# A graph and expert kernel on one core: GpSimd's row sum waits for one more VectorE step, and VectorE's list rows come ahead of its search

## What is computed

```python
x = x + _L0_gnn_ref(_layernorm(x), edge_index, ...)     # 8 heads of 64
x = x + _L0_ffn_ref(_layernorm(x)[None], ...)[0]        # 8 experts, top 1
x = x + _L1_gnn_ref(_layernorm(x), edge_index, W, b)
x = x + _L1_ffn_ref(_layernorm(x)[None], ...)[0]        # 64 experts

# end of the first graph step, for each node and head:
out = segment_sum(w[:, :, None] * x_l[src], dst)  # listed edges + the node's own loop
return elu(out + bias) + x
# first feed-forward step, for each node:
h = relu(xf @ W1[e] + b1[e]);  oe = h @ W2[e] + b2[e]
out = out + where(idx_k == e, gate_k * oe, 0.0)   # only the best expert's h counts
```

## Time and profile before

| | us |
|---|---|
| median of 3 runs | 2760.67 |
| lowest, highest | 2751.52, 2766.61 |
| profiled execution, its own time | 2749.01 |
| its span from first to last instruction | 2747.3 |
| first and last start of the wide sum L1072 | 1000.5, 1376.7 |

### The profile page before, as it was taken

The page is one execution under the profiler, slowest core; times in us unless marked ns, Lnnn a source line. Parts: engine busy times, 40 slices in busy tenths (PEclk is TensorE's granted clock), DMA queues, the critical chain, the costliest instruction groups (busy, mean ns, idle before and its releaser), DMA issues. The chain is left out here.

```text
span 2747.3 us, 43544 instructions
## 1 busy us (share of the span) xinstructions
PE 2127.1 (77%) x11528; PEld 1264.7 (46%) x11554; DVE 1834.1 (67%) x5188; ACT 928.1 (34%) x2017; POOL 1791.9 (65%) x2144
## 2 busy tenths in 40 slices
PE   8999999957777739999978969999997577774000
PEld 3444444435555526666644436666664344442000
DVE  5776676645555569999951126777778487776666
ACT  1111111115555515777764425555554000000000
POOL 3555555477777457888727745777777655664776
PEclk9999999978998959999989989999999799997555
DMA  6655555548999756888749976766663799997999
GB/s 199 230 192 179 185 192 181 183 155 280 309 305 306 245 160 199 254 262 265 244 164 361 403 270 206 213 218 218 216 212 104 229 358 382 373 352 257 381 385 353
DMA packets 361541, 699.30 MB, mean 255 GB/s; under 512 B 51513, under 2 KB 85139, under 8 KB 361297
## 3 DMA queue, kind: packets, MB, share of 16 engines
q1 hardware_dynamic: 239816, 399.95, 42.6%
q0 software_dynamic: 76720, 218.39, 24.3%
q10 hardware_dynamic: 44761, 78.17, 7.9%
HBM read 426.08 MB, written 287.44 MB: 260 GB/s over the span
## 5 line engine op out<-in xcount | busy, mean ns | idle before, releaser
L2119 POOL DMA_INDIRECT xg<-n_rows,ids x219 | 219.0, 1000 | 126.4 <-PE psum L154 78.4
L148 PE MATMUL psum<-wl,xT 128*128 128x512 f32 x632 | 288.8, 600 | 0.0
L148 PE MATMUL psum<-wg,yT 128*128 128x512 f32 x632 | 285.2, 594 | 0.0
L148 PE MATMUL psum<-wr,xT 128*128 128x512 f32 x632 | 284.1, 592 | 0.0
L337 ACT ACTIVATE xb<-xa,xsc 128x512 f32<-128x512 f32 x79 | 64.4, 817 | 479.6 <-POOL xsc L397 479.6
L154 PE MATMUL psum<-ident,xg 128*128 128x128 f32 x876 | 139.4, 298 | 103.9 <-DVE gT L2226 88.8
L384 POOL TENSOR_TENSOR ve<-mv,epst 128x1 f32<-128x1 f32 x79 | 51.0, 646 | 254.4 <-DVE mv L439 254.4
L1688 POOL DMA_INDIRECT slot_tokens<-sl x158 | 169.0, 1070 | 70.6 <-issue 66.9
L2285 POOL DMA_INDIRECT q<-slot_outputs,qs x158 | 165.1, 1045 | 72.0 <-issue 47.8
L148 PEld LDWEIGHTS psum<-wr,xT 128*128 128x128 f32 x632 | 120.1, 190 | 151.2 <-issue 151.2
L148 PE MATMUL psum<-wc,x1T 128*128 128x264 f32 x632 | 162.8, 402 | 32.1 <-DVE hb L1231 24.6
(11 more groups left out here) (322 smaller groups left out, 5329.1 us busy)
## 6 DMA issues: line engine op xcount, KB each, us to landing
slot_outputs<-yo ACTq DMA_DIRECT2D x54, 1024.0 KB
x_rows<-x SPq DMA_DIRECT2D x158, 256.0 KB, 3.2
edge_sums<-eo SPq DMA_DIRECT2D x29, 1056.0 KB, 6.7
edge_sums<-go SPq DMA_DIRECT2D x29, 1024.0 KB
xT<-in_xTt SPq DMA_DIRECT2D x79, 256.0 KB
xl_rows<-xl SPq DMA_DIRECT2D x79, 256.0 KB
xr_rows<-xr SPq DMA_DIRECT2D x79, 256.0 KB
residual_rows<-xb SPq DMA_DIRECT2D x79, 256.0 KB, 3.8
```

Source lines behind the costliest of these rows:

```text
L148: last = nc.tensor.matmul(ps, lhs[:, k, :], rhs[:, k, :], start=(k == 0), stop=(k == DK - 1))
L2119: pool.indirect_dma_start(xg[:, t % 8, :], None, XN3, bass.IndirectOffsetOnAxis(ids[:, t:t + 1], 0), bounds_check=NP - 1, oob_is_err=False ...
```

## The change

`average` gets a wait: from tile 9 on, the sum of tile t waits until `routed` of tile t-9 is through. Both VectorE steps, `self_part` of tile t and `routed` of tile t-9, belong to VectorE's turn t+2. And in VectorE's list `listed_part` moves from behind `best` to ahead of it, and `best` moves ahead of the two group steps `larger` and `slopes`. No instruction is added or taken away on any engine.

```diff
@@ average
                     pool.wait_ge(c_ta, t + 1)
                     pool.wait_ge(c_ts, t + 1)
+                    if t >= 9:
+                        pool.wait_ge(c_hm, t - 8)
                     if t >= 3:
                         pool.wait_ge(c_ex, t - 2)
                         pool.wait_ge(c_xq, t - 2)
@@ VectorE's list
                 tiles_in_turn(NT, (
-                    (11, hidden), (5, negative), (0, once(larger, 0)), (21, fourwise(slopes)), (11, best), (2, listed_part),
+                    (11, hidden), (5, negative), (2, listed_part), (11, best), (0, once(larger, 0)), (21, fourwise(slopes)),
                     (0, once(below, 0)), (21, fourwise(shifts)), (11, its_number), (2, self_part),
```

## The result

| | before | after |
|---|---|---|
| median (5 runs each) | 2760.67 | 2792.53 |
| lowest, highest | 2751.52, 2766.61 | 2791.48, 2793.07 |
| profiled execution, its own time | 2749.01 | 2792.53 |
| its span | 2747.3 | 2790.8 |
| first and last start of the wide sum | 1000.5, 1376.7 | 1000.3, 1420.6 |

The changed kernel takes 1.0117 of the time before (95% interval 1.0099 to 1.0136): slower by 31.9 us, where 36 were forecast. The profiled executions lie 43.5 us apart, and the stretch from the first sum to the last grew from 376.2 to 420.3 us, by 44.1: in the trace the whole loss lies in this stage.

The account below looks back on a forecast made before the run. VectorE was taken to set the pace, TensorE close behind. A hold of 65 us less 36 given back makes 29, plus 7 for the list is +36: 2785 us profiled, 2797 as median with 11.7 added; range 2776 to 2820.

Parts of the forecast that it names:

- The mechanism: The wide sum, released by `routed`, starts ahead of VectorE's `negative` and holds it; chance 0.70.
- L1262 near 420 ns: Sign in the changed kernel: `routed` is no longer held and has a mean near 420 ns.
- L1226's median near 1650: Sign in the changed kernel: `negative` is held and has a median near 1650 ns.
- 0.94 us a turn x 69 = 65: Loss at `negative`, held by the sum: a mean of 0.94 us in 69 turns, 65 us.
- The semaphore takes 0.15 us: Step at the new wait: the sum starts 0.15 us behind the end of `routed` (R).
- The 36 us given back: Gain on VectorE: 35.0 us at `routed` and about 1.1 at small step L1169, no longer held.
- The list, +7 us: VectorE's `its_number` directly behind `best`, whose result it needs: 0.12 us in each of 59 turns.
- The sum against the median: Whole kernel: 2785 us on the profiled execution, plus 11.7 for the median of the runs, gives 2797.
- Sum late or race lost: Rival: `negative` goes first; the sum holds `self_part` (2795 us, chance 0.09) or `listed_part` (2820 us, chance 0.06).
- L1224 not held: Rival: `negative` runs freely beside the sum, the turn falls to 4.70 us, 2739 us in all; chance 0.07.
- No change that can be told: Rival: `negative` held in only 16 to 46 of 69 turns, time within 0.5%, 14 us; chance 0.08.
- What would show it: Signs in the changed kernel's profile: step durations, sum's start and idle time, a 0.04 gap, 5.5 us turns, TensorE near 85%.

Follow-up runs that it names:

- e1: The kernel before with the new wait alone, VectorE's list as before: 2791.4 us, ratio 1.0132.
- e3: The changed kernel with the wide sum adding only columns 0 to 255 of each row: 2752.16 us, ratio 0.9985.
- e4: The changed kernel with `add_experts`, which reads PSUM, moved from ahead of `routed` to behind `hidden`: 2765.73 us, ratio 1.0035.
- e9: The kernel before with VectorE's list reordered, among others `add_experts` directly behind `positive` and `routed` a turn later behind `best`: 2858.41 us, ratio 0.9935.
- e7: The kernel before with an always satisfied wait added to the sum, on `routed` of tile t-10: 2882.63 us, ratio 0.9992.
- e5: The kernel before with `routed` moved to the next turn, behind `hidden` and `best`: 2886.92 us, ratio 1.002.
- e10: The kernel before with VectorE's list rewritten, TensorE's `turn_h` and `down` one turn later, ScalarE's `scaled` directly behind its exponential: 2758.61 us, ratio 0.9998.
- e2: The changed kernel without the new wait, so the new list order alone: 2783.51 us, ratio 1.0098.

## Why the prediction was right, and where its sizes were not

**The mechanism: right.** The sum follows `routed`, and `negative` is held in nearly every turn (e1 with the wait alone; e3 by length; e4 and e9 by PSUM steps). L1262 near 420 ns: 419. L1226's median near 1650: in the single lines of the changed kernel, 1020 to 1420 us, it is 1721:

```profile
L1226 DVE SCALAR_TENSOR_TENSOR x<-mi,xq x72: 682/1721/1970, 1021.3 to 1415.1; 128x512 f32<-128x512 f32 x72
...
L1074 POOL TENSOR_TENSOR oc<-ta,ts x72: 1257/1264/1603, 1020.8 to 1415.0; 128x512 f32<-128x512 f32 x72
```

**The term "0.94 us a turn x 69 = 65": too small.** It measured 70.2 / 69 = 1.02. The step in it that failed is "The semaphore takes 0.15 us": it was 0.23. All else in the chain held (`negative` due at R + 0.33, seen 0.32; end 0.55 behind the sum, seen 0.56), and 0.08 x 69 = 5.5 us is the difference. Why 0.23 is open. In e7, with one wait more, the sum still starts 0.15 behind `self_part`, so the number of waits isn't it; in e1 and e3, where `routed` releases it, it is 0.23 again in most turns.

**The 36 us given back: right.** 34.6 at L1262 and 1.0 at L1169/L1171.

**The list, +7 us: right only in this company.** The whole adds up: 70.2 - 34.6 - 1.0 + 7 = 41.6; `listed_part` (L1198) has 714 ns for L1196's 669, 3.6 us more, most of it in two turns in which it was held; `self_part` has 673 for 688, 1.2 less. That is 44.0, beside the 43.5 us between the spans and the 44.1 of the sum range; other groups of VectorE moved by less than 2 us each. Beside the wait the bubble is worth what was forecast, less what late sums take (of the 7 us, e1's sum range gives 4.4). By itself the same list costs 26 us, by way of a race that the forecast did not know of, since it took `one_hot` to escape. That reading was wrong, though no term of the sum rests on it. With the new wait the sum never comes to that seam.

**The sum against the median.** On the profiled execution I forecast 2785, and it was 2792.5, 7.5 low. The 11.7 us that I added for before's median did not come: the changed kernel's five runs lie within 1.6 us, its profiled one at their median, while those of the kernel before spread over 15. So 2797 was only 4.5 too high by luck: an offset that didn't carry over outweighed a hold that was sized too low. Which stage makes up before's 11.7 no trace shows.

**The rivals.** "Sum late or race lost": its condition was wrong in part. A sum that starts 0.31 us later than the forecast had it, behind a late transfer, still holds `negative` (12 turns of e1). The race was lost only once in each of the two kernels: in the changed one at 1319.72, with GpSimd idle before it, the sum came 0.53 behind R, `negative` went first in 0.68 us, and `listed_part` was held, as that rival said. "L1224 not held": excluded. "No change that can be told": excluded by the interval. **What would show it:** L1239 to L1244 have the gap, TensorE went to 83 for 85, the turn to 5.63 for 5.55. Two signs were wrong: the sum starts 0.23 and not 0.15 behind L1262, and its idle time reads "issue" and not VectorE's `hm`, which isn't explained.

## What to carry to other kernels

Where GpSimd runs a wide operation beside VectorE, don't ask when it may start but which VectorE steps stand under it: here steps that read PSUM were free, and a step with two inputs in SBUF paid what was left of the operation. A long duration of a step that is short at its minimum was a hold here, by the operation that ended 0.28 to 0.56 us before it; taking that one step away moves the hold to the next (e5), so place the whole length of the operation (e9), and then look at what the freed engine runs into: here a buffer ring read by ScalarE (e10), and TensorE. An order of steps is worth measuring by itself even where it should be neutral, since it can tip a race.

## What the runs showed of the hardware that I had not expected

- Two turns whose recorded starts agree to 0.02 us end differently (`one_hot` 0.28 and 1.36 us): at a seam between two adjacent two-input steps either the sum or the second step goes first.
- A sum that stands directly behind the transfer L1063 held `negative` although its recorded start was 0.13 us, once 0.79, behind that of `negative` (e1).
- The recorded start of a GpSimd instruction isn't when it gets the ports: its length over 1.26 to 1.28 us (2.07 in the earlier trace rows) is waiting inside the instruction.
- The held step ends 0.55 us (512 columns), 0.28 (256) or 0.14 (128) behind the sum, 0.13 to 0.14 less than its own 0.68, 0.41 and 0.28: either the ports are let go a little before the recorded end, or part of the step's start-up lies under it. No run tells these apart.
- Where nothing else keeps it back, the sum starts 0.15 us behind `self_part` (before, e2, e7) and 0.23 behind `routed` (the changed kernel, e1, e3).
